# Side work beside a causal attention: single places from a table in place of an even spread

## What is computed

```python
x = x + 0.5 * ffn(layernorm(x))
x = x + attn(layernorm(x))      # 16 heads of 16, causal over 4096 tokens
x = x + 0.5 * ffn(layernorm(x))
# ffn: x @ base_W.T + base_b + shared low-rank part (rank 16)
#      + 6 routed low-rank parts (rank 16), weighted by the top 2 of a softmax gate
# attn: k, q, v = x @ W.T; layernorm of q and k inside each head, scaled by 256**-0.25;
#       softmax(q k^T, causal) v, then @ Wo.T + bo
```

## Time and profile before

| | |
|---|---|
| median of three runs | 1289.55 us (1288.99 to 1294.87) |
| profiled execution, its own time | 1288.32 us |
| its span | 1286.5 us |
| PE / ACT / DVE / POOL busy | 1129.7 / 1018.6 / 471.1 / 242.9 us |
| mean granted TensorE clock | 0.966 |

### The profile page before, as it was taken

One profiled execution on the slowest core, in us unless ns is written; L12 is line 12 of the kernel. 1 busy time (PEld: TensorE's weight loads), 2 busy tenths in 40 slices (PEclk: granted clock), 3 DMA queues, 4 the chain that ended last, 5 costly groups with the idle time before them and its releaser, 6 DMA issues.

```text
span 1286.5 us, 22763 instructions
## 1 busy us (share of the span) xinstructions
PE 1129.7 (88%) x8884; PEld 361.6 (28%) x8884; DVE 471.1 (37%) x1177; ACT 1018.6 (79%) x1135; POOL 242.9 (19%) x377
## 2 busy tenths in 40 slices
PE   2646868899899999999999999999999999999994
PEld 2432322323233322323223222223222222222223
DVE  4655645445355434343333332332322212021104
ACT  3203546768988799888998999998999999999990
POOL 2223433222322131121112202111202101010100
PEclk9777899999999999999999999999999999999996
DMA  5011200200300030000300002100001200000000
GB/s 136 2 39 45 83 2 18 67 1 18 99 3 1 18 93 9 1 1 26 92 2 1 1 9 78 32 1 1 2 4 33 65 1 1 9 9 1 1 17 17
DMA packets 39672, 33.37 MB, mean 26 GB/s; under 512 B 8786, under 2 KB 39496, under 8 KB 39560
## 3 DMA queue, kind: packets, MB, share of 16 engines
q1 hardware_dynamic: 37360, 31.74, 8.4%
q10 hardware_dynamic: 2200, 0.12, 0.1%
HBM read 18.73 MB, written 12.85 MB: 25 GB/s over the span
## 4 chain that ended last, share of the span: by engine, by line
PE 59%; ACT 18%; DVE 11%; issue 8%; POOL 2%; ACTq 1%; SPq 0%; DMA 0%; DVEq 0%; POOLq 0%
PE ps L1136 56%; ACT ring L729 17%; PE ps L1178 2%; PE ps L1244 1%; DVE xnT L1124 1%; DVE xnT L801 1%; DVE st L760 1%; POOL ring L683 1%; DVE area L1120 1%; DVE oT L1105 1%; PE ps L1198 1%; DVE xnT L1122 1%; DVE area L781 1%; POOL rstd L670 0%; DVE xnT L799 0%
## 5 line engine op out<-in xcount | busy, mean ns | idle before, releaser
L729 ACT ACTIVATE ring<-ps 128x1024 f32<-128x1024 f32 x1056 | 985.4, 1126 | 129.9 <-PE ps L1136 128.4
L1136 PE MATMUL ps<-ring,vf 128*17 128x512 f32 (+3 forms) x4608 | 561.6, 564 | 8.3 <-POOL ring L683 6.9
L1136 PE MATMUL ps<-queries,keys 50*128 50x512 f16 (+3 forms) x2304 | 378.8, 369 | 49.5 <-ACT ring L729 16.5
L1136 PEld LDWEIGHTS ps<-queries,keys 50*128 50x128 f16 x2304 | 93.8, 93 | 519.7 <-ACT ring L729 458.7
L683 POOL TENSOR_SCALAR_AFFINE_SELECT ring<-ring 128x256 f32<-128x256 f32 (+1 forms) x224 | 105.3, 489 | 434.3 <-ACT ring L729 432.0
L1136 PEld LDWEIGHTS ps<-ring,vf 128*17 128x17 f32 x4608 | 80.0, 95 | 177.0 <-issue 145.4
L1105 DVE STREAM_TRANSPOSE oT<-ps 128x512 f32<-128x512 f32 x32 | 22.9, 716 | 155.3 <-PE ps L1136 155.2
L799 DVE CAST xnT<-ps 128x512 f16<-128x512 f32 x32 | 22.0, 688 | 138.1 <-PE ps L1178 138.1
L670 POOL TENSOR_TENSOR rstd<-var,minus_half 128x4 f32<-128x4 f32 x24 | 24.4, 1018 | 253.7 <-DVE var L766 253.5
L933 DVE SCALAR_TENSOR_TENSOR x<-ps,power,x 128x512 f32<-128x512 f32 x32 | 23.9, 750 | 113.0 <-PE ps L1136 113.0
L1136 PE MATMUL ps<-baseT,xnT 128*128 128x256 f16 x384 | 55.8, 286 | 4.0 <-DVE wf L807 1.4
(11 more groups left out here) (150 smaller groups left out, 673.7 us busy)
## 6 DMA issues: line engine op xcount, KB each, us to landing
parts_d<-split SPq DMA_DIRECT2D x32, 256.0 KB, 2.6
keys<-parts_d SPq DMA_DIRECT2D x96, 64.0 KB, 2.3
queries<-parts_d SPq DMA_DIRECT2D x192, 32.0 KB
x<-in_x SPq DMA_DIRECT2D x8, 512.0 KB, 4.4
out_x<-x SPq DMA_DIRECT2D x16, 256.0 KB, 2.2
queries<-shift_d SPq DMA_DIRECT2D x64, 4.0 KB
ring<-in_base_W SPq DMA_DIRECT2D x1, 256.0 KB, 4.6
ring<-in_Wq SPq DMA_DIRECT2D x1, 256.0 KB, 6.1
```

Of the source, the lines that this page charges most:

```text
L729: act.activation(probs[:, u % RING, :], bank(2 * (u % SLOTS), 2), ACTF.Exp, bias=0.0, scale=1.0).then_inc(exp_ok, 1)
L1136: return pe.matmul(o, lhsT, rhs, start=start, stop=stop, skip_group_check=True)
```

## The change

The side items keep their kinds, their number and, within each of the four lists, their order. Where each of them stands among the units now comes from a table, `PLACES`, with one whole number per item: place 3u, 3u+1 or 3u+2, counted from the first unit of the chunk. Place 3u comes after exp and mask and before scores(u+2), place 3u+1 after the divide and before `values`, place 3u+2 at the end of the unit, where all side items stood before. Place -1, used by the first 15 items of `prepare(1)`, is ahead of `scores` 0. A cut of the diff (other rows of the table are of the same kind; those of the later chunks span the whole chunk):

```diff
+def side_work(c):
+    if c + 1 < NC:
+        yield "prep", list(itertools.chain(front(0, 0, c + 1) if c >= LONG else (), prepare(c + 1)))
+    if c + 2 <= LONG:
+        yield "ff", list(front(0, 0, c + 2))
+    if c >= 1:
+        yield "out", list(output(c - 1))
+    behind = [c - 2] if 2 <= c < NC - 1 else [c - 2, c - 1] if c == NC - 1 else []
+    if behind:
+        yield "back", list(itertools.chain(*map(back, behind)))
...
+PLACES = {
+        (0, "prep"): (-1, -1, -1, -1, -1, -1, -1, -1, -1, -1, -1, -1, -1, -1, -1, 0, 1, 2, 3, 4, 4, 4, 7, 7, 8, 19, 19, 19, 21, 25, 36, 43),
+        (0, "ff"): (0, 2, 6, 9, 14, 19, 27, 30, 33, 36, 37, 46, 49, 55),
+        (1, "prep"): (0, 3, 5, 10, 12, 18, 18, 24, 28, 30, 34, 34, 42, 44, 44, 48, 61, 61, 61, 67, 79, 79, 79, 90, 90, 90, 92, 92, 100, 101, 126,
+        134),
+        (1, "ff"): (17, 21, 22, 32, 36, 51, 56, 59, 96, 107, 120, 129, 147, 152),
+        (1, "out"): (35, 60, 63, 81),
+        (2, "prep"): (0, 14, 20, 22, 23, 29, 49, 53, 55, 59, 59, 59, 65, 72, 81, 84, 96, 103, 104, 128, 135, 137, 138, 138, 156, 157, 167, 167, 178,
+        201, 223, 245),
+        (2, "out"): (19, 27, 42, 48),
+        (2, "back"): (50, 51, 55, 74, 74, 97, 129, 137, 145, 149, 153, 166, 185, 191, 232),
...
+        (6, "prep"): (33, 44, 61, 61, 77, 100, 121, 135, 136, 142, 144, 156, 167, 190, 192, 195, 221, 226, 260, 277, 280, 299, 310, 324, 336, 346,
+        350, 355, 355, 380, 389, 408, 410, 452, 461, 463, 467, 482, 492, 496, 496, 505, 518, 562, 595, 624),
...
+}
...
+    side = {}
+    for c in range(NC):
+        for name, items in side_work(c):
+            for (_, stage, n), place in zip(items, PLACES[c, name], strict=True):
+                side.setdefault(3 * UNIT0[c] + place, []).append((stage, n))
+    yield from side.pop(-1, [])
     yield "scores", 0
     yield "scores", 1
-    side = {}
-    for c in range(NC):
...
-            lists.append(spread(itertools.chain(ahead, prepare(c + 1)), u0 + 6 if c >= LONG else u0, max(u1 - 12, u0 + 6)))
...
-            lists.append(spread(output(c - 1), u0 + 4, u0 + 8))
...
     for u in range(NU):
         yield "exp", u
         if UNITS[u][3] is not None:
             yield "mask", u
+        yield from beside(3 * u)
         if u + 2 < NU:
             yield from scores(u + 2)
             yield from fetch_ready()
...
+        yield from beside(3 * u + 1)
         while values and values[0][0] <= u:
...
-        for stage, n in side[u]:
-            yield stage, n
-            if stage == "heads" and n[1] >= 2:
-                split.add((n[0], n[1] - 2))
-                yield from fetch_ready()
+        yield from beside(3 * u + 2)
```

More of the change, by code:

```diff
@@ L169, in together @@
             yield from s.get(k, [])
+PLACES = {
[9 more added lines that the diff above has]
+        (2, "back"): (50, 51, 55, 74, 74, 97, 129, 137, 145, 149, 153, 166, 185, 191, 232),
+        (3, "prep"): (12, 40, 40, 42, 48, 53, 66, 71, 78, 78, 83, 89, 99, 104, 145, 157, 163, 165, 165, 177, 186, 186, 192, 195, 202, 202, 203, 209,
+        220, 220, 220, 228, 232, 249, 249, 249, 249, 262, 262, 273, 276, 283, 284, 295, 319, 339),
+        (3, "out"): (13, 18, 29, 42),
+        (3, "back"): (44, 58, 58, 58, 78, 127, 146, 184, 216, 231, 231, 240, 250, 271, 287),
+        (4, "prep"): (6, 28, 28, 42, 54, 70, 82, 121, 123, 130, 133, 139, 151, 163, 164, 164, 164, 164, 183, 188, 199, 206, 220, 224, 231, 233, 233,
+        239, 253, 256, 257, 267, 268, 297, 299, 302, 306, 317, 318, 324, 324, 324, 368, 377, 405, 437),
+        (4, "out"): (5, 14, 28, 36),
+        (4, "back"): (38, 43, 48, 66, 94, 106, 117, 197, 222, 237, 271, 282, 299, 339, 349),
+        (5, "prep"): (0, 17, 61, 62, 65, 78, 92, 97, 101, 102, 102, 114, 125, 143, 148, 148, 148, 189, 225, 235, 255, 255, 269, 275, 293, 302, 302,
+        311, 321, 323, 340, 342, 343, 354, 354, 354, 356, 385, 402, 404, 404, 426, 434, 445, 462, 527),
+        (5, "out"): (8, 18, 29, 47),
+        (5, "back"): (48, 88, 107, 166, 171, 181, 204, 282, 302, 310, 318, 367, 411, 509, 522),
+        (6, "prep"): (33, 44, 61, 61, 77, 100, 121, 135, 136, 142, 144, 156, 167, 190, 192, 195, 221, 226, 260, 277, 280, 299, 310, 324, 336, 346,
+        350, 355, 355, 380, 389, 408, 410, 452, 461, 463, 467, 482, 492, 496, 496, 505, 518, 562, 595, 624),
+        (6, "out"): (12, 20, 32, 55),
+        (6, "back"): (73, 78, 112, 128, 138, 213, 238, 293, 322, 323, 338, 435, 452, 540, 633),
+        (7, "out"): (21, 43, 45, 97),
+        (7, "back"): (98, 119, 122, 122, 137, 164, 181, 182, 190, 211, 281, 295, 336, 371, 380, 388, 388, 388, 395, 449, 466, 553, 561, 562, 581, 615,
+        615, 666, 696, 710),
+}
@@ L178, in schedule @@
                 yield "fetch", (0, 2 * (n[1] - 2) + g)
+    side = {}
[4 more added lines that the diff above has]
+    yield from side.pop(-1, [])
     yield "scores", 0
     yield "scores", 1
-    side = {}
-    for c in range(NC):
-        lists = []
-        u0, u1 = UNIT0[c], UNIT0[c + 1]
-        if c + 1 < NC:
-            ahead = front(0, 0, c + 1) if c >= LONG else ()
-            lists.append(spread(itertools.chain(ahead, prepare(c + 1)), u0 + 6 if c >= LONG else u0, max(u1 - 12, u0 + 6)))
-        if c + 2 <= LONG:
-            lists.append(spread(front(0, 0, c + 2), u0, u1 - 2))
-        if c >= 1:
-            lists.append(spread(output(c - 1), u0 + 4, u0 + 8))
-        behind = [c - 2] if 2 <= c < NC - 1 else [c - 2, c - 1] if c == NC - 1 else []
-        if behind:
-            lists.append(spread(itertools.chain(*map(back, behind)), u0 + 10, u1 - 2 if c == NC - 1 else u1 - 20))
-        for u in range(UNIT0[c], UNIT0[c + 1]):
-            side[u] = [q for steps in lists for q in steps.get(u, [])]
     values, groups, scored, split = [], [], set(), set()
@@ L209, in fetch_ready, with beside @@
             yield "fetch", fetches.pop(0)
+    def beside(place):
+        for stage, n in side.get(place, []):
+            yield stage, n
+            if stage == "heads" and n[1] >= 2:
+                split.add((n[0], n[1] - 2))
+                yield from fetch_ready()
     for u in range(NU):
```

## The result

The changed kernel takes 1210.7 us (median of 4 runs, 1209.4 to 1212.2) against 1290.2 for the kernel before: a ratio of 0.938, 95% interval 0.935 to 0.940. It is 6.2% faster. I had forecast 1262, with a range from 1242 to 1281: the direction was right, and the size was a third of what was measured.

The account below looks back on a forecast made before the run. PE was taken to set the pace up to chunk 6 (73.8 us idle) and ACT beside chunk 7 (7.1 us idle). Terms A to F summed to -27 us from 1288.3, giving 1261.3, forecast as 1262, range 1242 to 1281.

Parts of the forecast that it names:

- A: Start: 15 items of prepare(1) ahead of the first scores fill PE's wait for queries; -6 us, bounds nothing to 9 gained.
- B: Rest of chunk 0: the wait behind the roots and the adjacent pairs go; -5 us, bounds 0 and 11.
- no wait over 2 us on PE beside chunks 0 to 2: Sign expected in the changed profile: beside chunks 0 to 2 PE has no wait longer than 2 us.
- Term F: Chunk 7: ACT is 98% busy, so at most 7.1 us can be had; -1 us, bounds -4 and +2.
- C: Beside chunk 1: waits of 2.92 and 1.75 us and four pairs go; -6 us, bounds 3 lost, 13 gained.
- D: Beside chunk 2: the 2.90 us wait at a qk goes; -3 us, bounds -6 and +2.
- E: Beside chunks 3 to 6: work reaches the chunk's end, with better spacing; -6 us, bounds 4 lost, 16 gained.
- Only the start moves: Rival: chunks 2 to 7 stay as before; A, B and half of C remain, -14 us, 1275; chance 0.15.
- No net effect: Rival: scores' later start is paid in full and spacing returns only as much; 1289 us; chance 0.05.
- The stalls and the half clock both go: Rival: clock full from about 100 us on, C and E near their bounds; -48 us, 1241; chance 0.14.
- The slower rival: Clumps of roots or norms on DVE stall PE in seven places, costing 23 us; +9 us, 1298; chance 0.06.

Follow-up runs that it names:

- e15: Changed kernel with the first two routes of each chunk from 3 on moved to the place of the inner ahead of them; 1236.1 us, ratio 0.957.
- e7: Changed kernel, but beside chunks 3 to 6 the old even spread, stretched to the chunk's end; 1264.3 us, ratio 0.979.
- e7b: As e7, with the load of x right behind the last outer and both lists ended a little earlier; 1250.2 us, ratio 0.968.
- e18: Changed kernel with only the back lists at their old even spread; 1235.7 us, ratio 0.954.
- e16: Changed kernel with only the four items of each output list back at their old units; 1239.1 us, ratio 0.960.
- e4: Changed kernel's table beside chunks 3 to 7 only, the even spread of before beside chunks 0 to 2; 1263.3 us, ratio 0.978.
- e9: Changed kernel, but beside chunks 3 to 7 the lists merged in old order and spaced evenly by PE time, at units' ends; 1252.0 us, ratio 0.969.
- e3: Changed kernel's table beside chunks 0 to 2 only, the even spread of before beside chunks 3 to 7; 1245.8 us, ratio 0.963.
- e1: Kernel before with only the first 15 items of prepare(1) moved ahead of the first scores; 1290.5 us, ratio 0.997.
- e5: Changed kernel with each item at its unit's end and DVE instead of ACT reading side items' banks beside chunk 1; 1238.2 us, ratio 0.959.
- e6: Changed kernel with its table in full, DVE instead of ACT reading side items' banks beside chunk 1; 1213.9 us, ratio 0.940.
- e13: As e9, but with a share of the units for every item, not for PE's alone; 1236.0 us, ratio 0.958.

## Why the prediction was wrong

**What held.** The start: the first exp near 103 (103.2), the DMA wait gone, three qk ahead of the scores, the end unchanged (33.3 and 33.2). A and B together: -11 forecast for start and chunk 0, -13.5 measured (chunk 1's first exp at 143.0 against 156.5; near 145 was forecast). The sign "no wait over 2 us on PE beside chunks 0 to 2" held but for one of 2.2 us. Term F: -1, measured -2.8, within its bounds.

**What failed: terms C, D and E.** C was -6 with a bound of -13 and is -24.4. D was -3, bound -6, and is -9.1. E was -6, bound -16, and is -27.9. Of the 51 us by which the sum was short of the spans' difference, these make 18, 6 and 22.

The first step that failed is "No order of the side items can do away with work. What it can do away with is PE's idle time". Half of it is wrong. PE's busy time up to chunk 6 fell by 27.9 us. Of these 8.2 moved into the startup. Of the other 19.7, 8.8 fell beside chunks 3 to 6, where the clock is full before and after, and 10.9 beside chunks 0 to 2, where part of it was time at half clock. Beside chunk 1, by line, before and then after:

```profile
L1136 PE MATMUL ps<-queries,keys 50*128 50x512 f16 (+3 forms) x130 | 19.9, 354 | 6.6 <-ACT ring L729 6.4
L1136 PE MATMUL ps<-woT,xnT 128*128 128x256 f16 x24 | 4.2, 346 | 1.8 <-DVE xnT L801 1.8
```

```profile
L1179 PE MATMUL ps<-queries,keys 50*128 50x512 f16 (+3 forms) x128 | 17.5, 342 | 0.5 <-ACT ring L772 0.2
L1179 PE MATMUL ps<-woT,xnT 128*128 128x256 f16 x24 | 3.0, 273 | 0.0
```

And the scores beside chunk 6, at full clock before and after:

```profile
L1136 PE MATMUL ps<-queries,keys 50*128 50x512 f16 (+1 forms) x448 | 74.6, 373 | 7.1 <-ACT ring L729 2.0
L1179 PE MATMUL ps<-queries,keys 50*128 50x512 f16 (+1 forms) x450 | 74.1, 373 | 3.6 <-ACT ring L772 0.5
```

At full clock the single matmul is no shorter, 373 ns in both. Busy time is the time in which at least one matmul runs; the matmuls of this kernel overlap in the profile, and with fewer waits between them they overlap more. With C's idle time of 18.5 as a ceiling, no share of it could have reached 24.4.

The second is "PE is the busier engine up to chunk 6 and therefore sets the pace there". PE and ACT hand units to each other with a lead of two or so, and a wait of ACT was not made up even where PE is the busier: e15 took nothing from PE's queue, ACT waited 24.0 us in ten places, and the kernel was 25 us longer. ACT's busy time beside the chunks hardly moved (996.9 and 991.7 us), so the ceiling that holds is ACT's idle time in the earlier trace rows, 160.6 us; half of it went.

The third is the share, and it weighs most: of the 46 us by which C, D and E were short, 29 are idle time of PE that I had counted but left standing, and 17.5 are the busy time. I took a third, a third and a fifth of the idle time, named waits one by one, and priced an adjacent pair at 0.69. The table removed nearly all: 18.5 to 1.2, 9.4 to 2.0, 28.9 to 9.7. The wait of 1.75 us at a projout, which I added to C at its face value, is the tail of a longer stall: with the old output lists in the table the whole chunk is 10.6 us longer. And within E the reason is not borne out: it had 5 of its 6 us from the filled ends, and these were neither confirmed nor refuted (e7, e7b), while the lists' places cost 16.4 (e18) and 11.2 us (e16) in the same four chunks.

A reading was wrong as well, without a consequence for the sum: PE is at 9 tenths from the ninth slice on, with an 8 at the eleventh, not between 2 and 8 in the first ten.

**The rivals.** "Only the start moves" is excluded by e4 (0.978 without the start). "No net effect" did not occur. "The stalls and the half clock both go", with 0.14, named the right mechanism and still stopped at 1241, since it was built on PE's idle time too; the smaller part of the gain is the clock's, as shown below. The slower rival named a real mechanism: clumps do cost, on ACT (e9, e15) more than on DVE. The table has triple roots in three units and pays nothing visible for them: PE's waits for gathers (DVE oT) beside chunks 0 to 2 are 0.7 us in all. That nothing which PE needs soon stands behind them is my reading.

**The clock.** After the change, by stretch:

```profile
88.50:108.90 20.40, 13.69 (x72) 6.97 (x72) 10.98 (x34) 7.03 (x10) 10.58 (x11) 0.75 0.34 94
117.30:124.10 6.80, 6.71 (x42) 3.61 (x43) 4.50 (x8) 2.83 (x3) 4.04 (x7) 0.52 0.12 41
134.40:137.80 3.40, 3.40 (x27) 1.86 (x20) 0.51 (x1) 2.64 (x3) 2.93 (x7) 0.54 0.44 134
```

The first stretch is half at full clock, two short ones are left behind it, and beside chunk 1 the mean granted clock is 1.00 instead of 0.96. From the first exp to the last, 37.1 us stood at half clock before and 10.2 do now, all of them beside chunk 0. By the page's rule in the Trainium skill that I cited ("TensorE: Matmul & The Clock Gate", section "HAM oscillation — how this bites in real kernels"), up to 15 us, an estimate by that rule, hung on the two stretches at 1.2 GHz.

What the clock costs by itself can be read where the same order ran at another clock. Beside chunk 3, e3 has the order of before; its row answers to the one of 345.00:475.10 in the earlier trace rows, and the second row is its stretch at half clock:

```profile
299.70:432.60 132.90, 125.61 (x1014) 40.36 (x1010) 60.77 (x145) 109.63 (x119) 30.82 (x45) 0.97 0.13 38
405.60:412.40 6.80, 6.15 (x34) 1.71 (x34) 1.48 (x3) 2.14 (x3) 3.62 (x7) 0.50 0.11 39
```

PE's longest waits are the same in both (2.7, 1.2, 0.9 us), PE is busy 3.0 us longer, and the chunk takes 2.8 us more. In the same way e1 takes 2.9 us more beside chunk 2 with 6.8 us more at half clock, and 0.9 and 1.5 us more beside chunks 1 and 3 with 3.4 each. At 0.26 to 0.44 us for each us at half clock, the 26.9 us fewer are worth 7 to 12 us, by my estimate, of the 77.6. The page's rule, a loss of half the throttled time, points the right way; these rows give somewhat less. None of it lies beside chunks 3 to 7, where neither trace has a stretch at half clock.

**Open.** Which single places carry the rest of chunk 1, and why the unit's end costs 13.9 us there; e5 and e6 did not settle it. What the filled ends are worth, and what the `prep` lists' places are. How the table was found is not known, and no rule that I tried reaches it: the best, e13, takes 671.8 us where it takes 647.8.

## What to carry to other kernels

Where two engines hand work to each other through few buffers, count the idle time of both before setting a ceiling for a new order, and take that of the engine whose busy time an order cannot change (here ACT); busy time of the matmul engine is not a floor. Place every side item by when its producer is done, in the queue of each engine that it visits: the 0.22 us instruction at the head of ACT's queue cost some 2.5 us in each of ten places, and four items of one output list at their old units made one chunk 10.6 us longer. Before drawing out a list, look at what its last item feeds (here the load of x).

## What the runs showed of the hardware that I had not expected

A single wait of PE can be followed by matmuls at the clock's lower level. The 24 projout matmuls beside chunk 1 have a mean of 346 ns before and 273 after. With the old output lists in the table, the projout behind the wait of 5.24 us took 2.74 us at a granted clock of 0.5 and the next one 1.50, so that this wait cost another 1.24 us in the item behind it alone. It is not so behind every wait: in the trace of before PE waits 2.65 us for a mask at 451.55 (beside chunk 3), and the granted clock stays full.

Over the whole kernel the same 2304 scores matmuls were busy for 378.8 us before and 363.0 after, while their mean length is 369 and 366 ns: busy time of PE is a result of the order, too, and a busy share near 1 does not say that the engine has no time to give.
